# Rounding step of an int8 quantization: the doubling is folded into a ScalarE instruction

## The reference

```python
# attention, 16 heads of 64
attn = 1.0 + s + 0.5 * s * s          # s = (q * d**-0.5) @ k.T, causal mask to 0
o = (attn @ v) / (sum(attn) + EPS)
x = layernorm(x + y @ Wo.T)
# quantized linear layer
amax = max(abs(x), axis=-1)
x_scale = maximum(amax, EPS) / 127.0
x_q = clip(round(x / x_scale), -128, 127).astype(int8)
acc = dot(x_q, weight_q.T)            # int32
x = layernorm(x + acc * x_scale * weight_scale + bias)
```

## Time and profile before

| | |
|---|---|
| time, median of 2 runs | 995.84 us (995.67 to 996.02) |
| time of the profiled execution | 995.53 us |
| span of its slowest core (core 1) | 993.9 us |
| spans of the 8 cores | 984.7 to 993.9 us |
| granted TensorE clock, mean | 0.817 to 0.828 |
| quantization loop, core 1 | about 758 to 890 us |

### The profile page before, as it was taken

The page is one execution under the profiler, slowest core; times in us unless marked ns, Lnnn a source line. Parts: engine busy times, 40 slices in busy tenths (PEclk is TensorE's granted clock), DMA queues, the critical chain, the costliest instruction groups (busy, mean ns, idle before and its releaser), DMA issues.

```text
span 993.9 us, 8874 instructions; the slowest of 8 cores (984.7 to 993.9 us)
## 1 busy us (share of the span) xinstructions
PE 620.2 (62%) x2688; PEld 223.2 (22%) x2688; DVE 489.7 (49%) x793; ACT 410.9 (41%) x435; POOL 111.3 (11%) x100
## 2 busy tenths in 40 slices
PE   1249859929978777777868777743991111129910
PEld 0014314404422222221222122211440000014400
DVE  0003203302345656656566565643897666657752
ACT  0000000000059888887889797850232333332310
POOL 1100010011000000000000000001003555540000
PEclk9999959958979889887899897985896555559965
DMA  5640230145000110101010111115440000000025
GB/s 108 108 82 1 31 54 1 22 64 85 1 0 1 23 32 24 32 23 33 23 33 23 32 22 34 28 39 157 139 148 21 1 0 1 0 1 1 1 115 222
DMA packets 14833, 43.89 MB, mean 44 GB/s; under 512 B 2244, under 2 KB 2756, under 8 KB 13764
## 3 DMA queue, kind: packets, MB, share of 16 engines
q0 software_dynamic: 8192, 23.07, 12.1%
q1 hardware_dynamic: 6596, 20.25, 6.1%
HBM read 44.11 MB, written 8.52 MB: 53 GB/s over the span
## 4 chain that ended last, share of the span: by engine, by line
PE 32%; DVE 20%; DMA 18%; ACT 17%; issue 10%; POOL 0%; DVEq 0%; ACTq 0%; POOLq 0%; SPq 0%
ACT uab L462 14%; PE pq L235 9%; PE oab L505 8%; DMA wbuf<-wqt 6%; PE pa L798 6%; PE pv L289 6%; PE ps L442 4%; DVE t L716 3%; DMA wbuf<-wkt 3%; DMA wbuf<-wvt 3%; DVE xq L736 2%; DVE ot_fin L375 2%; DVE x L605 2%; DVE uab L470 2%; ACT t L725 2%
## 5 line engine op out<-in xcount | busy, mean ns | idle before, releaser
L462 ACT ACTIVATE uab<-ps,consts 128x1024 f16<-128x1024 f32 (+1 forms) x320 | 322.0, 1085 | 56.1 <-PE ps L442 56.1
L505 PE MATMUL oab<-uab,vz 128*65 128x512 f16 (+3 forms) x640 | 195.8, 391 | 61.5 <-DVE uab L485 31.1
L235 PE MATMUL pq<-xTsb,wbuf 128*128 128x512 f16 x512 | 126.7, 410 | 70.1 <-DMA wbuf<-wqt 53.8
L442 PE MATMUL ps<-qT,kT 64*128 64x512 f16 (+3 forms) x640 | 125.6, 389 | 23.3 <-ACT uab L462 21.3
L485 DVE TENSOR_SCALAR uab<-uab 128x1024 f16<-128x1024 f16 x192 | 79.3, 422 | 104.8 <-ACT uab L462 104.8
L462 ACT ACT_TABLE_LOAD x1 | 1.3, 1283 | 281.5 <-PE ps L442 281.5
L767 PE MATMUL pt<-ident_sb,xq 128*128 128x128 f16 x128 | 16.2, 306 | 126.1 <-DVE xq L736 126.1
L235 PEld LDWEIGHTS pq<-xTsb,wbuf 128*128 128x128 f16 x512 | 51.1, 102 | 145.2 <-issue 93.1
L505 PEld LDWEIGHTS oab<-uab,vz 128*65 128x65 f16 x640 | 48.2, 116 | 143.8 <-issue 143.0
L597 PE MATMUL py<-woT,ot_fin 128*128 128x512 f16 x256 | 61.6, 407 | 25.1 <-DMA ot_fin<-ob_tmp 25.1
L470 DVE SCALAR_TENSOR_TENSOR uab<-uab,tri_sb 128x256 f16<-128x256 f16 x128 | 54.5, 426 | 44.1 <-ACT uab L462 42.5
(11 more groups left out here) (67 smaller groups left out, 477.7 us busy)
## 6 DMA issues: line engine op xcount, KB each, us to landing
rzb<-rzscr POOLq DMA_DIRECT2D x16, 512.0 KB, 4.6
xs<-x_tok SPq DMA_DIRECT2D x16, 512.0 KB
xTsb<-xT POOLq DMA_DIRECT2D x8, 512.0 KB, 5.5
out<-xs SPq DMA_DIRECT2D x8, 512.0 KB
out<-t SPq DMA_DIRECT2D x8, 512.0 KB
wbuf<-wqt POOLq DMA_DIRECT2D x8, 256.0 KB, 6.3
wbuf<-wkt POOLq DMA_DIRECT2D x8, 256.0 KB, 3.6
wbuf<-wvt POOLq DMA_DIRECT2D x8, 256.0 KB, 3.5
```

The costliest lines, as they stand in the source:

```text
L235: return t.matmul(ps[:, qcc * 512:(qcc + 1) * 512], lhs, rhs, start=(fi == 0), stop=(fi == NCH - 1))
L442: return t.matmul(ps[:, ab * 512 + js: ab * 512 + 512], lhs, rhs, start=True, stop=True, tile_position=(r0, 0))
L462: return s.activation(dst, src, AF.Square, bias=c_rs, scale=c_rs)
L505: return t.matmul(ob[0:65, ab * 512 + js: ab * 512 + 512], lhs, rhs, start=(kt == 0), stop=(kt == 4 * qc + 3))
```

## The change

The ScalarE instruction of line 725 now computes 2 * er - 2 * MAGIC in place of er - MAGIC, and writes the result as int32 into `g32`. The VectorE instruction of line 729 is gone. The addition into `xq` (line 736, now 732) waits for ScalarE's count where it waited for VectorE's. Nothing else is edited; lines behind it carry numbers smaller by 4.

```diff
         def mkm2(s, t=t):
-            return s.activation(er[t % 2][:, :], er[t % 2][:, :], AF.Copy,
-                                bias=-MAGIC)
+            return s.activation(g32[t % 2], er[t % 2][:, :], AF.Copy,
+                                bias=-2.0 * MAGIC, scale=2.0)
         plan.op("scalar", mkm2, waits=[(sSc, sSc.n)], incs=[(sSc, 1)])
-        def mkg(v, t=t):
-            return v.tensor_scalar(g32[t % 2], er[t % 2][:, :],
-                                   2.0, None, ALU.mult)
-        plan.op("vector", mkg, waits=[(sSc, sSc.n)], incs=[(sDV, 1)])
-        wv = [(sDV, sDV.n)]
+        wv = [(sSc, sSc.n)]
         if t >= 2:
             wv.append((sPE, tr_done[t - 2]))
```

## The result

The changed kernel takes 982.38 us (median of 11 runs, 978.71 to 990.31), the kernel before took 995.8 us (median of 10). The ratio is 0.9874 with a 95% interval of 0.9847 to 0.99: 1.3% faster, and clear of no change. 983.0 us was forecast. The profiled execution took 982.02 us, its slowest core (core 5) spans 980.3 us.

The account below looks back on a forecast made before the run. The quantization loop was taken as bound by each tile's latency chain through VectorE and ScalarE. 995.53 - 12.8 (16 x 0.80) = 982.7 us, plus 0.3 us for the median, gives 983.0 us; range 980 to 987.5 us.

Parts of the forecast that it names:

- The bound: Quantization loop: a chain of waits through VectorE and ScalarE, each tile costing its whole latency, 8.14 to 8.21 us, 16 times.
- The removed term: Line 729's place in each tile's chain, from its start to the addition's: 0.80 us, 16 times, 12.8 us saved.
- The second wait: The addition also waits for the transposes of two tiles before; 0.07 us a tile, left in from tile 2 on.
- The unknown price: Line 725 writing int32, which no ScalarE instruction of the trace did; taken as nothing, at most 0.91 us more per tile.
- Rival 1: The int32 output makes line 725 slower, 997.5 us at factor 1.86; 4% for a loss, 4% for a partial price.
- Rival 2: The earlier addition runs into GpSimd's line 757 and takes 2031 ns, losing all of the gain: 995.8 us; chance 3%.
- What is late next: After the doubling goes, nothing else needs longer than the tile's 7.34 us; GpSimd needs under 5 us per tile.
- Rival 3: The doubling was hidden by another equally long chain per tile, so the change does nothing: 995.8 us; chance 1%.

## Why the prediction was right

- **The bound.** The loop was read as a chain of latencies that repeats 16 times. Both undoing one half and doing the other half elsewhere confirm it: with the instruction 8.21 us a tile, without it 7.41, wherever the doubling went.
- **The removed term.** 16 x 0.80 = 12.8 us were forecast; the loop became 12.86 us shorter, for the reason given. That the median then came out 0.6 us from the forecast is in part luck, as said above.
- **The second wait.** The 0.07 us that were left in from tile 2 on were measured in the changed kernel (0.17 against 0.10 us), and went away with the wait.
- **The unknown price.** Taking nothing for the int32 output was right: 1057 ns against 1058. Rival 1 is out.
- **Rival 2** did not occur, for the reason given, the gap of 0.26 to 0.32 us. But its price was wrong. A collision does not turn 1226 ns into 2031; the addition is held to the end of GpSimd's instruction and then needs 1.08 us, which made 2.42 us in one kernel and 3.37 in another. The prediction noted the 2031 ns of the subtraction only as a warning for the addition, and did not draw that the subtraction was losing 0.80 us a tile already, in both kernels.
- **What is late next.** GpSimd, with under 5 us of its own, was taken as free up to 7.34 us. That is right for the serial loop and would have misled for the next step: its time and VectorE's cannot be laid side by side.
- **Rival 3** is out by the same runs as the first point. No step of the sum failed.

## What to carry to other kernels

Where a loop is a chain through two engines and back, an instruction on it costs its full distance to the next start, and it does not matter which neighbour takes over its arithmetic. Before reordering such a loop for overlap, check whether two of its engines can overlap at all: equal instructions with unequal times are the sign, and an instruction that ends a fixed time after its neighbour's is the proof. Then what the same edit is worth depends on the bound: 12.9 us in the chain, 6.8 us where another engine's pace lies close below. And a tile picked from a trace should be compared with its neighbours: the single tiles with a gap of 0.46 us are not the pace of their loops.

## What the runs showed of the hardware

- A VectorE instruction with its inputs in SBUF that meets a running GpSimd instruction ends here 1.08 us (two inputs, 128x1024) or 0.54 to 0.55 us (one float32 input) after GpSimd's end, and counts as busy all the while. One-input instructions are struck too: line 705 took 2.65 us in place of 0.81, the cast 1.47 in place of 0.69, the doubling 2.83 in place of 0.69. A two-input one that reads one of its inputs from PSUM was not (1.27 us).
- It works both ways: GpSimd's tensor addition took 2.34 us alone and 3.13 us behind VectorE's subtraction, its scalar form 1.20 and 1.69.
- ScalarE's time for 128x1024 was 1056 to 1059 ns with float32 and int32 output and with the three sets of constants used here; the Identity function with scale and bias read per partition took 1243 ns.
- VectorE did an addition and a subtraction of constants in one instruction of 694 ns, as much as a cast or a multiplication alone, and a scalar factor ahead of a two-input addition cost nothing (1226 ns).
- A wait long met cost 0.07 us when it stood second at VectorE's addition (0.17 us from release to start against 0.10).
